# Two stage boundaries of a twelve-layer kernel: the quantised layers' preparation made inside the folded attention, the gated scan's weights loaded inside the context attention

## The reference

```python
xc, z = jnp.split(x @ W_in, 2, axis=-1)
xt = conv_general_dilated(xt, conv_w, ..., feature_group_count=D_INNER)   # 4 taps
u = silu(xt);  dt_raw, B_raw = split(u @ W_x, 2);  dt = softplus(dt_raw @ W_dt + b_dt)
h = h * (1 - d_t) + u_t * (B_raw @ W_Bp)          # along the sequence
y = (h + D_param * u) * silu(z);  return y @ W_out
```

```python
q = (x @ Wq + bq).reshape(b, h, dh, t)            # k and v alike: a fold, not a transpose
attn = softmax(einsum('bhdt,bhds->bhts', k, v) * temperature)
out = einsum('bhdt,bhts->bhds', q, attn)
# quantised feed-forward
scale = maximum(max(abs(x)), 1e-6) / 127;  xq = round(x / scale)
out = (matmul(xq, wq.T) + b) * (sw * sx)          # for w1, then gelu, then for w2
```

## Time and profile before

| | |
|---|---|
| median of three runs | 3559.14 us |
| profiled execution | 3559.38 us, its span 3557.5 us |
| PE busy | 3208.9 us (90%) |
| DVE busy | 2507.1 us (70%) |
| ACT busy | 1835.4 us (52%) |
| POOL busy | 1260.3 us (35%) |
| mean granted clock of PE | 0.941 of full speed |

### The profile page before, as it was taken

The page is one execution under the profiler, slowest core; times in us unless marked ns, Lnnn a source line. Parts: engine busy times, 40 slices in busy tenths (PEclk is TensorE's granted clock), DMA queues, the critical chain, the costliest instruction groups (busy, mean ns, idle before and its releaser), DMA issues. The chain is left out here.

```text
span 3557.5 us, 110134 instructions
## 1 busy us (share of the span) xinstructions
PE 3208.9 (90%) x41582; PEld 2687.3 (76%) x41584; DVE 2507.1 (70%) x7190; ACT 1835.4 (52%) x4594; POOL 1260.3 (35%) x1887
## 2 busy tenths in 40 slices
PE   6886999999989999888899999999999999873866
PEld 4665999999957777546789889888998899743345
DVE  6784999999968888567455555555555555477765
ACT  4341777787768888574433333333333333343463
POOL 3673888888834343204200000000000000174042
PEclk8996999999989999998799999999999999997677
DMA  4001000000022222100465555555555555374000
GB/s 121 8 2 40 1 0 0 0 0 0 1 70 82 82 83 81 46 1 7 99 145 130 126 127 139 127 130 132 132 131 127 127 136 130 74 134 62 0 3 27
DMA packets 375654, 254.59 MB, mean 72 GB/s; under 512 B 118724, under 2 KB 371608, under 8 KB 374680
## 3 DMA queue, kind: packets, MB, share of 16 engines
q1 hardware_dynamic: 370968, 245.64, 28.4%
q10 hardware_dynamic: 4352, 4.20, 0.5%
HBM read 233.73 MB, written 15.75 MB: 70 GB/s over the span
## 5 line engine op out<-in xcount | busy, mean ns | idle before, releaser
L2482 PE MATMUL psum<-L_xattn_ctxT,L_xattn_q_ctx 128*128 128x257 f32 x2048 | 508.8, 389 | 2.9 <-issue 2.3
L1076 PE MATMUL psum<-L_ffn_share,L_ffn_prob 128*128 128x128 f32 x4096 | 487.9, 278 | 23.1 <-DVE L_ffn_prob L1009 15.6
L893 POOL TENSOR_TENSOR L_ffn_sums<-L_ffn_sims 128x1024 f32<-128x1024 f32 x256 | 485.4, 1913 | 61.2 <-DVE L_ffn_prob L1009 61.2
L2513 PEld LDWEIGHTS psum<-L_xattn_probT,L_xattn_ctx 32*128 32x128 f32 x16384 | 468.9, 187 | 44.5 <-issue 42.0
L1076 PEld LDWEIGHTS psum<-L_ffn_share,L_ffn_prob 128*128 128x128 f32 x4096 | 471.3, 193 | 35.8 <-DVE L_ffn_prob L1009 25.6
L2513 PE MATMUL psum<-L_xattn_probT,L_xattn_ctx 32*128 32x128 f32 x16384 | 493.2, 273 | 2.1 <-DVE L_xattn_probT L2396 2.1
L2334 ACT ACTIVATE L_xattn_prob<-psum,L_xattn_nmax 128x258 f32<-128x258 f32 x512 | 239.2, 472 | 479.9 <-DVE L_xattn_nmax L2382 463.0
L2305 POOL TENSOR_TENSOR L_xattn_z_var<-L_xattn_z_mv,L_xattn_z_eps 128x1 f32<-128x1 f32 x32 | 6.1, 192 | 1245.0 <-DVE L_xattn_z_mv L2408 1215.7
L2482 PEld LDWEIGHTS psum<-L_xattn_ctxT,L_xattn_q_ctx 128*128 128x128 f32 x2048 | 367.3, 190 | 64.8 <-issue 8.2
L935 ACT ACTIVATE psum<-L_ffn_sums,L_ffn_bias 128x512 f32<-128x512 f32 x512 | 339.1, 686 | 64.8 <-DVE L_ffn_prob L1009 60.3
L1009 DVE SCALAR_TENSOR_TENSOR L_ffn_prob<-L_ffn_sums,L_ffn_best,psum 128x512 f32<-128x512 f32 x512 | 358.1, 741 | 7.0 <-ACT psum L935 3.4
(11 more groups left out here) (463 smaller groups left out, 6504.0 us busy)
## 6 DMA issues: line engine op xcount, KB each, us to landing
L_xattn_ctx<-ctx_dram SPq DMA_DIRECT2D x512, 256.0 KB, 3.8
L_xattn_ctxT<-ctx_T_dram SPq DMA_DIRECT2D x128, 257.0 KB, 3.3
L_xattn_k_all<-ctx_T_dram SPq DMA_DIRECT2D x128, 128.5 KB, 2.1
L_xattn_v_all<-ctx_dram SPq DMA_DIRECT2D x128, 128.0 KB, 2.2
L_attn_qkv_scratch<-L_attn_qkv SPq DMA_DIRECT2D x24, 256.0 KB, 3.2
L_attn_rows<-L_attn_qkv_scratch SPq DMA_DIRECT2D x24, 256.0 KB, 5.3
start_raw<-ctx_dram ACTq DMA_DIRECT2D x16, 256.0 KB, 11.9
L_xattn_v_rows<-L_xattn_v SPq DMA_DIRECT2D x8, 256.0 KB, 2.3
```

The costliest lines, as they stand in the source:

```text
L893: nc.gpsimd.tensor_tensor(sums[:, h % RING, :, :], sx, sy, ALU.add).then_inc(summed, 1)
L1076: last = nc.tensor.matmul(pair(2 * s)[:, c * P:(c + 1) * P], prob[:, h % RING, c * P:(c + 1) * P], share[:, h % RING, :], start=(h == 0 an ...
L2482: last = nc.tensor.matmul(scores(s)[:, g, 0:CTX], q_ctx[:, p, c, b, h:h + 4, :].rearrange("p h n -> p (h n)"), ctxT[:, b, c, :], start=(c ...
L2513: last = nc.tensor.matmul(mix_bank(r)[:, c * P:(c + 1) * P], ctx[rows, b, k, c * P:(c + 1) * P], probT[rows, b % 2, k, :, :].rearrange("p ...
```

## The change

Two pairs of functions now share what the second of them needs. `context_and_gated` and `folded_and_quantised` make an object with the buffers and semaphores of the second function's preparation, and hand it to both.

- `GatedWeights`: the 13 loads stand in SP's list of the context attention, between its loop (now one round shorter) and the loads of the last tile; the four products on POOL stand at the end of POOL's list there.
- `QuantisedFront`: the weights' and biases' loads follow the folded attention's own at the start of SP's list; the greatest magnitudes of the weights stand behind the first bias addition of the projection on DVE, the split of the bias behind the third; the six small stores stand in SP's list behind the store of step 1, their load back behind SP's loop. `back` is now the q part of `qkv`. At the end DVE adds and makes moments in six parts of 4, 8, 8, 4, 4 and 4 tiles; the last two parts are normalised by DVE rather than by ACT; and the weights are rounded last, after the step of `x`.

```diff
+class QuantisedFront:
+    PARTS = (range(0, 4), range(4, 12), range(12, 20), range(20, 24), range(24, 28), range(28, 32))
+    BY_ACT = 4
+    def sp_send_parts(self, sp):
+        sp.wait_ge(self.parts_done, 3)
+        for i in range(3):
+            sp.dma_start(self.bias_dram[i:i + 1, 0:H].rearrange("a (p j) -> (a p) j", j=C), self.b_part[:, i, 0:C]).then_inc(
+                self.parts_out, 16)
+            sp.dma_start(self.bias_dram[i:i + 1, H:H + D].rearrange("a (p j) -> (a p) j", j=1),
+                         self.b_part[:, i, C:self.N_BIAS]).then_inc(self.parts_out, 16)
+    def pool_factors(self, pool):
+        for k, part in enumerate(self.PARTS):
+            self.front.pool_rstd(pool, 0, only=part)
+            if k < self.BY_ACT:
+                self.front.pool_shift(pool, self.shifted, part).then_inc(self.centred, 1)
...
@@ context_attention, SP
-            with sp.Fori(0, TILES - 1) as t:
+            with sp.Fori(0, TILES - 2) as t:
+                load_following(t)
+            gated.sp_load(sp)
+            load_following(TILES - 2)
@@ context_attention, POOL
+            gated.pool_clear(pool)
...
             over_tiles(pool, tile)
+            gated.pool_scale(pool)
@@ folded_attention, SP
+            quant.sp_load(sp)
             for n in range(STEPS):
                 store_qkv(n)
...
             store_res(1, 1)
+            quant.sp_send_parts(sp)
             load_back(0, 0, back_in)
...
+            quant.sp_load_parts(sp)
             for n in (STEPS - 2, STEPS - 1):
@@ folded_attention, DVE
+                if live(1) and not live(2):
+                    quant.dve_weight_peaks(dve)
+                if live(3) and not live(4):
+                    quant.dve_split_bias(dve)
...
-            dve.wait_ge(back_in, 16 * (STEPS - 1))
-            most = slice(0, TILES - S)
-            nc.vector.tensor_tensor(core.x[:, most, :], core.x[:, most, :], back[:, most, :], ALU.add)
+            dve.wait_ge(back_in, 16 * (STEPS - 2))
+            for part in quant.PARTS[0:4]:
+                add_back(part[0], part[-1] + 1)
+                quant.dve_moments(dve, part)
+            dve.wait_ge(mid_in, 16)
+            add_back(TILES - 2 * S, TILES - S)
+            quant.dve_moments(dve, quant.PARTS[4])
             dve.wait_ge(last_in, 16)
-            rest = slice(TILES - S, TILES)
-            nc.vector.tensor_tensor(core.x[:, rest, :], core.x[:, rest, :], back[:, rest, :], ALU.add)
+            add_back(TILES - S, TILES)
+            quant.dve_moments(dve, quant.PARTS[5])
+            quant.dve_greatest(dve, 1, 3, 1)
+            quant.dve_peak(dve, 0)
+            quant.dve_peak(dve, 1)
+            quant.dve_steps(dve, 1, 3, 1)
+            for k in (4, 5):
+                quant.dve_normalise(dve, k)
+            quant.dve_peak(dve, 2)
+            quant.dve_peak(dve, 3)
+            quant.dve_own_peak(dve, 4)
+            quant.dve_own_peak(dve, 5)
+            quant.dve_step_x(dve)
+            quant.dve_round_weights(dve)
@@ program
-            lambda: context_attention(core, "L1_xattn"),
-            lambda: gated_scan(core, "L1_attn"),
+            lambda: context_and_gated(core, "L1_xattn", "L1_attn"),
...
-            lambda: folded_attention(core, "L2_attn"),
-            lambda: quantised_ffn(core, "L2_ffn"),
+            lambda: folded_and_quantised(core, "L2_attn", "L2_ffn"),
```

More of the change, by code:

```diff
@@ L1860, in _, with context_and_gated @@
                     widen(t - 1)
+def context_and_gated(core, cross, gated):
+    with ExitStack() as st:
+        weights = GatedWeights(core, st, gated)
+        context_attention(core, cross, weights)
+        gated_scan(core, gated, weights)
 def ternary_ffn(core, name):
@@ L2593, in folded_attention @@
         res = sb("res", [P, B, SEQ])
-        back = sb("back", [P, TILES, D])
+        back = qkv[:, :, 0, :]
         bank_a = lambda s: core.psum[:, 2 * s, :]
@@ L2902, in _ @@
-        @block.gpsimd
-        def _(pool):
-            for c in chunks:
-                front.pool_rstd(pool, 0, only=c)
-                front.pool_shift(pool, shifted, c).then_inc(centred, 1)
+        (x_rounded, turned, qT_done, wide, gelued, peaks_h, h_rounded, turned2, hT_done, out_done, added) = (
+            core.sem(f"{name}_{n}") for n in (
+                "x_rounded", "turned", "qT_done", "wide", "gelued", "peaks_h", "h_rounded", "turned2", "hT_done", "out_done", "added"))
+        block = st.enter_context(nc.Block())
@@ L2980, in _ @@
-            front.dve_moments(dve, 0, only=chunks[3])
-            nc.vector.tensor_copy(ones_b[:, :], core.ones[0:3, :])
-            steps_of(1, 3, 1)
-            peak_of(0)
-            peak_of(1)
-            round_weights()
-            peak_of(2)
-            peak_of(3)
-            dve.drain()
-            nc.vector.tensor_reduce(peaks[:, 0:1], peak_x[:, :], X, ALU.max).then_inc(peaks_x, 1)
-            greatest(0, 1, 2)
-            steps_of(0, 1, 2)
-            nc.vector.tensor_tensor(scale[:, 0:1], most[:, 0:1], most[:, 1:2], ALU.mult)
```

330 lines of the change are left out of this document (180 added, 150 removed).

## The result

| | before | after |
|---|---|---|
| median | 3558.84 us (3550.21 to 3559.98, 15 runs) | 3563.74 us (3557.52 to 3568.51, 15 runs) |
| ratio | | 1.0016, interval 1.0008 to 1.0023 |
| profiled execution | 3559.38 us | 3558.21 us, span 3556.4 us |

The kernel became 5.7 us slower by the ratio, where the forecast was 3556 us, 0.1% less, with 3563 as the upper end of its range. The profiled execution of after lies among the shortest of its 15, so the two profiles are compared stretch by stretch and not by their totals.

A forecast was written before the change was run, and what follows sets the result against it. It took stretches where PE stands still at two boundaries as the limit, following DVE at the second. Terms -14.4 + 2.7 + 7.1 + 0.5 - 5.3 + 4.8 + 1.2 = -3.4 from 3559.38 gave 3556 us, range 3547.5 to 3563.

The forecast's parts named there:

- The quantised front: At the second boundary, DVE would round the first tiles at 3273.9 instead of 3288.33: 14.4 us saved, given 13 to 15.5.
- DVE's work in the projection: In the folded attention's projection, weights' magnitudes, split and copy delay DVE's chain: 2.7 us lost, at most 3.1.
- The gated scan's start: At the first boundary, DVE no longer waits for loads, so PE's convolution starts earlier: 5.3 us saved.
- The 13 loads: In the context attention they delay the last tile's keys: 4.8 us lost, plus 1.2 for PE's clock falling.
- The small stores: In the folded attention they hold step 4's rows, stalling POOL at tile 16: 7.1 us lost, plus 0.5 for PE's clock.
- what is issued behind lands behind: On SP's queue, step 4's rows would land behind the small stores, not before 3204.0, 7.1 us after POOL wants them.
- The rival with longer stores: Same stall at POOL's tile 16, stores slower among traffic, last landing 19.0 after issue: 3571.5 us, 0.35% slower; chance 0.12.
- Writes to one short row: Argument against longer small stores: 250 KB loads spread over other addresses should not slow such writes much.

The follow-up runs named there:

- experiment 8: Kernel after with the six small stores behind the projection's first store_qkv, SP waiting until they are written before issuing anything else: 0.9983 of before.
- experiments 5: Kernel after with each partition's piece of the six small stores in its own 512-byte stretch of scratch, read back by two loads: 0.9977 of before.
- 9: Kernel without small stores, gated weights behind the last keys, plus twelve unread stores of 128 pieces at various strides, SP waiting for each: landings 1.4 to 18.1 us.
- 11: Kernel after with only the three stores of 2-byte pieces changed, pieces 64 bytes apart, the 8-byte ones left side by side: 0.9969 of before.
- experiments 3: Kernel after with the six small stores moved behind the projection's first store_qkv, the load back keeping its place: 0.9985 of before.
- 7: Kernel after with the same six small stores issued by ACT behind its exponential of tile 7, instead of by SP: 1.0012 of before.
- experiment 1: Kernel after with the six small stores and their load back moved behind the last load_back of the folded attention's SP list: 0.9965 of before.
- experiment 12: Kernel without small stores, gated weights behind the last keys, plus one unread side-by-side 2-byte store behind the first store_qkv, SP waiting: 3544.46 us, 0.9953 of before.

## Why the prediction was wrong

The forecast was 3556 us, in a range from 3547.5 to 3563, by gains of 19.7 and losses of 16.3; measured were 3563.74, and by the ratio 5.7 more than before. One loss, that of the small stores, was put at less than half of what it measured. By the prediction's own steps:

- **The quantised front, 14.4 saved: right.** D went from 43.4 to 29.1 in every kernel with the move.
- **DVE's work in the projection, 2.7 lost: right.** B grew by 2.9 in after, by 2.1 to 3.4 in the others without an early store. No run takes DVE's new work out of the projection, so that it is the cause rests on the forecast's argument.
- **The gated scan's start, 5.3 saved: right,** 5.3 (13.94 to 8.69); the products were hidden.
- **The 13 loads, 4.8 and 1.2 lost: right in kind.** The wait was 4.99 and A grew by 7.0 against 6.0, the 1.0 coming behind the wait; PE's granted clock fell to 0.50 from 1448 to 1452, as forecast. Put elsewhere the loads gave 5.3 back by the ratios.
- **The small stores, 7.1 and 0.5 lost: the step that failed.** The mechanism and the place were the forecast's (the mask of tile 16 behind a load of rows), but C grew by 16.1. The rule "what is issued behind lands behind" was taken to mean that the rows would be landed the moment the last small store is. The rows came 25.9 after the first small store (3210.48 - 3184.57) where the forecast had 18.3 (3204.0 - 3185.66). The stores took about 1.5 of these 7.6 more (they held everything to 3204.4, 19.8), and about 6 are the third load's own way: SP, held for 14 us in the issue of the second, issued it only at 3203.69, and it took 6.7. The forecast let all three loads land with the last small store. Another 1.4 of C's 16.1 comes behind the mask, which was 14.7 late, where the forecast had 0.5 for the clock; PE had 0.50 until 3212 at least. So the 7.1 and 0.5 measured 14.7 and 1.4.

The sum of the measured terms is -14.4 + 2.9 + 16.1 - 5.3 + 7.0 = +6.3 against 5.7 by the ratio. The rival with longer stores named the right sign by the wrong mechanism: it asked for a last store 19.0 under way, and it had some 16.9 (3204.4 - 3187.48, if the stand-still ended with the landing, which the trace of after doesn't record). The stores take as long in quiet (18.3 before, from 3264.57 to SP's fetch at 3282.89, and 19.2 in experiment 8, against 19.8 here); they are slow because their pieces stand side by side (experiments 5, 9 and 11). "Writes to one short row" was put there as a reason against it, and is the cause.

The error of method lies in the bound. The nearest row, the third store's 10.3 behind one of 9.2, had been read as "held", but not asked why 256 bytes should need 9.2 and 1 KB only 2.8: a price that grows as the bytes shrink tells of something other than queueing, and that something could hold whatever else used the memory.

What stays open: what makes all engines stand still. It was there with six small stores side by side in every place where the engines exchange signals fast (after, experiments 3, 7 and 8; in 7 the late notice of the rows accounts for it), it ended 17.6 to 21.7 after the first issue (in experiment 8, which shows the landing, 0.6 ahead of SP's next issue), and it was absent with the pieces apart, the 2-byte ones alone included (experiment 11). That the late signals are PE's fits the rows of experiments 3 and 8, that they are a transfer's fits experiment 7; what the two have in common no run shows. Nor is it shown whether a memory line is being rewritten, as theory P's words have it: the runs show the dependence on the stride, not the mechanism behind it.

## What to carry to other kernels

Don't write pieces of a few bytes side by side to memory from many partitions: let each piece start 32 bytes or more behind the one before, join them to one longer piece per partition, or turn them on PE, which cost nothing here. Before work is moved to fill a stall, ask what the moved transfers do to those around them in the new place; behind the last transfer that anyone waited for the six slow stores cost nothing (experiment 1), in the midst of a stream they cost 16 us, and alone on the queue among fast exchanges of signals some 4 (experiment 8). And put loads that are needed later behind those that are needed next: the same 13 loads cost 6 us ahead of the last tile's keys and nearly nothing behind them.

## What the runs showed of the hardware

- A store of 128 pieces lands in 1.4 us where the pieces stand 32 bytes or more apart (from start to start), in 2.1 at 16 bytes, 2.8 to 3.0 at 8 (4.2 once, just behind larger loads), 18.1 to 18.2 at 2, be they 8 or 2 bytes long (3.4 once at 512 bytes, right behind the slowest one). Three of each, side by side, take 18 to 20 from the first issue.
- While six such stores are under way, loads behind them crawl (after: 14 to 21 GB/s for the core instead of over 100 just after) and an issue held SP for 14 us. The completion of transfers issued before them on another queue came late by some 13 us (experiment 7: all data there by 3184, taken up at 3197.2).
- With six of them under way each engine stood still for 3 to 13 us (experiment 8: 3.39 and 4.06; after: 10.51 to 12.65), and for DVE and ACT no releaser in the profile accounts for it. With one of them under way there was one pause of 1.6 (experiment 12).
